# Both output gates multiplied into the weights on GpSimd, instead of into the results on VectorE

## The chip, the cores and the metric

The kernel runs on one core of a Trainium2 chip. A core has TensorE (matrix products, the rows call it PE, its weight loads PEld), VectorE (DVE), ScalarE (ACT), GpSimd (POOL) and SyncE (SP, here only a queue for transfers). Each runs its own list of instructions in order, and they meet through semaphores. The metric is the time of one execution in device microseconds; the median of several executions is compared.

## The reference

One block of a transformer with adaptive layer norms over 8 images of 256 tokens, 256 channels:

```
mod = (silu(c) @ wmod) as (8, 6, 1, 256);  sa, ca, ga, sb, cb, gb = mod[:, 0..5]
ga, gb = sign * max(|.|, 0.25)                      # the two gates, one row of 256 per image
h = layernorm(x) * (1 + ca) + sa
x = x + ga * attention(h)                           # linear attention, 16 heads, chunks of 128
h = layernorm(x) * (1 + cb) + sb
x = x + gb * (routed_moe(h) + shared(h))            # 64 experts, 6 of them per token
attention(h) ends in: rmsnorm(rmsnorm(o) * norm_w) * proj_norm_w @ ternary(proj_w).T
shared(h) = (silu(h @ ws_gate) * (h @ ws_up)) @ ws_down
```

A gate scales the columns of a projection's result. `gate * (o @ W)` equals `o @ (W * gate)` with the gate along W's columns; on this the change rests.

## The kernel before, in words

The kernel has a prologue (constants, ternary weights, modulation rows), the token loop, the expert pairs, and a last stage that sums the six expert rows of each token.

The token loop handles one image of 256 tokens per step, in two tiles of 128 tokens, and is pipelined over images by hand: in step s, TensorE projects q, k, v of image s, forms the scores and values of its two tiles, projects the attention output of image s-1 (`project_out`, L1250 to 1257), transposes the normalised x2 of image s-1 (`norm2_transpose`, L1301), computes router logits (L1310), shared gate/up (L1322), and the shared down projection of image s-2 (`shared_down`, L1331). Each engine has its own `step` function, and the order of the calls in it is the order of execution. All order is written out by hand; nothing is scheduled by a program.

VectorE's step (L995 to 1035) is: routing scores of image s-2, `shared_out(s-3)`, statistics of the next image, `shared`, `out_norms(s-1)`, routing choice, `rms`, mask of tile 0 (`mask`, L844), `state_block`, `residual(s-1)`, `norm1_apply(s+1)`, the second layer norm of image s-1 (z), mask of tile 1, slots. The two functions that the change touches:

- `residual(b)` (L821 to 835) forms x2 = x + ga * fac * projection. It waits for `fac` (the factor of both rms norms, from GpSimd) and for the projection in the PSUM bank `ps_a`. Two instructions (L829, one per tile) multiply the bank by fac and by the gate row `mod_b[:, 0]`; one (L833) adds x, which is held in `pre`. Then `norm_stats` takes statistics of x2 (L669, L674, L677). GpSimd's `power` (L421) turns the variance into rstd, VectorE applies it (L683), and TensorE's transposes wait for that.
- `shared_out(b)` (L921 to 930) forms pre = x2 + gb * shared result. One instruction (L926) multiplies the PSUM bank by the gate rows `gb_all[:, b]` into `sh_g`, a second (L929) adds x2. The expert part is multiplied by gb in the last stage (L1105), in both kernels.

GpSimd's step (L447 to 457) is: rstd of the next image's first norm, `fac`, `q_lam` (L453), rstd of the second norm, and `norm2_rows` (L433, L435), which writes the normalised rows that the experts will gather. SP loads `mod_b` for an image (L317; three rows of 256, spread over 128 partitions, two buffers) and `gb_all` once (L322). `proj_done`, `dn_done`, `h2_ready` and the like are semaphores named for what they announce.

Of the kernel before, what the change touches and what calls it, by code (L numbers as in the profile page):

```python
# [66 lines left out]
def adaln_attention_moe(nc, x, qkv_w, qkv_norm_w, proj_w, proj_norm_w, norm_w, s, gate_w, bias,  # L67
                        w_gate, w_up, w_down, ws_gate, ws_up, ws_down, c, wmod, out):
    with ExitStack() as ctx:
        def sb(name, shape, dt=F32):  # L70
            return ctx.enter_context(nc.sbuf_tensor(name, shape, dt))
# [20 lines left out]
        pick_key = sb("pick_key", [P, B, NT * TOPK], BF16)  # L92
        neg_t = sb("neg_t", [P, T])
        decay = sb("decay", [P, 4, KC, 2, T])
# [7 lines left out]
        w_qkv = sb("w_qkv", [P, KC, 3 * C])  # L102
        w_proj = sb("w_proj", [P, KC, C])
        norm_cols = sb("norm_cols", [P, KC, 3])
        q_scale = sb("q_scale", [P, 2, KC])
# [61 lines left out]
        carry = sb("carry", [P, NT, E], BF16)  # L167
        w_raw = sb("w_raw", [P, NT, E])
        w_sum = sb("w_sum", [P, NT])
        w_rec = sb("w_rec", [P, NT])  # L170
# [30 lines left out]
        wcol = [wcols[:, i:i + 1] for i in range(WBUF)]  # L201

        spare = scm[:].rearrange("p r j q t -> p (r j q t)")
        xr = ([big[:, KEYS * i:KEYS * (i + 1)] for big in (spare, decay[:].rearrange("p r j q t -> p (r j q t)"))
# [45 lines left out]
        v_taken kt_done rr_a rr2_ready eps_ready klam_ready qlam_ready kv_done state_ready sc  # L250
        mk pv o_taken os_done f5 f_ready proj_done attn_ready x2_ready ln2_ve ln2_rstd
        z2_ready h2_mul h2_ready h2t_done h2T_ready lg_done lg_exp r1 selbf_ready w_step w_ready
        carry_ready gu_done sg_exp sg1 sh_ready dn_done sh_gated pre_ready pos_done slots_ready hot_ready ramp_ready inv_done picks_added
        unramped ix_ready xtp
# [113 lines left out]
        def _(pool):  # L368
# [15 lines left out]
            g.iota(neg_left[:], pattern=[[0, 1]], base=-T, channel_multiplier=1, allow_small_or_imprecise_dtypes=True)  # L384
            g.iota(neg_t[:], pattern=[[-1, T]], base=0, channel_multiplier=0, allow_small_or_imprecise_dtypes=True)
            g.iota(part_ix[:], pattern=[[0, 1]], base=0, channel_multiplier=1)
# [40 lines left out]
            def norm2_rows(b):  # L427
# [7 lines left out]
                g.tensor_tensor(rows, rows, spread(mod_b[b % 2][:, 1], 1, NT), ALU.add).then_inc(S["h2_ready"], 1)  # L435

            def unramp_table():

                g.memset(unramp[:], 0.0).then_inc(S["c_const"], 1)
                for i, f in enumerate((1.0, -2.0, 1.0)):  # L440
                    pool.wait_ge(S["c_const"], 11 + i)
                    g.affine_select(out=unramp[:], in_=unramp[:], pattern=[[1, P]], compare_op=ALU.not_equal, fill=f,
                                    base=-i, channel_multiplier=-1).then_inc(S["c_const"], 1)

            def step(s):
# [8 lines left out]
                if s >= 1:  # L454
                    power(rstd2[:], ve2[:], 0, "ln2_ve", "ln2_rstd", s)
                    norm2_rows(s - 1)

            pool.wait_ge(S["c_lam"], 1)
# [5 lines left out]
            power(rstd2[:], ve2[:], 0, "ln2_ve", "ln2_rstd", B)  # L464
            norm2_rows(B - 1)


# [31 lines left out]
        def _(act):  # L499
# [18 lines left out]
            for j in range(KC):  # L518
                a.activation(lam_q[:, j], neg_t[:], ACT.Exp, scale=s_part[:, j:j + 1])
            a.activation(lam_rev[:], s_row[:], ACT.Exp, scale=neg_left[:, 0:1]).then_inc(S["c_lam"], 1)  # L520
# [138 lines left out]
        def _(dve):  # L659
# [161 lines left out]

            def residual(b, par, hb):

                dve.wait_ge(S["f_ready"], b + 1)
                dve.wait_ge(S["proj_done"], b + 1)
                seen(dve, S["pre_ready"], b - 1)
                dve.wait_ge(S[f"ld_modb{par}"], 16 * (hb + 1))
                for i in range(NT):
                    last = v.scalar_tensor_tensor(out=x2[par][:, i], in0=ps_a[:, C * i:C * i + C], scalar=fac[:, i:i + 1],  # L829
                                                  in1=mod_b[par][:, 0], op0=ALU.mult, op1=ALU.mult)  # L830
                last.then_inc(S["attn_ready"], 1)
                dve.wait_ge(S["attn_ready"], b + 1)
                v.tensor_tensor(x2[par][:], x2[par][:], x_all[:, NT * b:NT * b + NT], ALU.add).then_inc(S["x2_ready"], 1)  # L833
                dve.wait_ge(S["x2_ready"], b + 1)
                norm_stats(b, [x2[par][:, i] for i in range(NT)], bn2, mv2, ve2, "ln2")
# [85 lines left out]
            def shared_out(b, par):  # L921

                dve.wait_ge(S["dn_done"], b + 1)
                dve.wait_ge(S["ld_gb"], 16)
                seen(dve, S["pre_ready"], b)
                v.tensor_tensor(sh_g[:], shared_bank(b)[:, 0:NT * C].rearrange("p (i c) -> p i c", i=NT), spread(gb_all[:, b], 1, NT),  # L926
                                ALU.mult).then_inc(S["sh_gated"], 1)
                dve.wait_ge(S["sh_gated"], b + 1)
                v.tensor_tensor(pre[:, NT * b:NT * b + NT], sh_g[:], x2[par][:], ALU.add).then_inc(S["pre_ready"], 1)  # L929

# [65 lines left out]
            def step(s, par, h, hp):  # L996
# [23 lines left out]
                if has_prev:  # L1020
                    residual(s - 1, 1 - par, hp)
                if nxt:
# [18 lines left out]
            token_steps(step, B - 1)  # L1041
            par, hb = (B - 1) % 2, (B - 1) // 2
            router_scores(B - 2)
            out_norms(B - 1, par)
            shared_out(B - 3, par)
            residual(B - 1, par, hb)
            shared(B - 2)
# [65 lines left out]
        def _(pe):  # L1113
# [76 lines left out]
            def project_qkv(b):  # L1190
# [8 lines left out]
                seen(pe, S["lg_exp"], b - 1)  # L1199
                seen(pe, S["sh_gated"], b - 2)  # L1200
                seen(pe, S["state_ready"], b)
# [47 lines left out]

            def project_out(b):  # L1250
                pe.wait_ge(S["rr_a"], min(b + 2, B))
                pe.wait_ge(S["klam_ready"], min(b + 2, B))
                for i in range(NT):
                    for k in range(KC):
                        last = mm.matmul(ps_a[:, C * i:C * i + C], oT[:, i, k], w_proj[:, k],
                                        start=(k == 0), stop=(k == KC - 1))
                last.then_inc(S["proj_done"], 1)
# [46 lines left out]
            def logits(b):  # L1304
                pe.wait_ge(S["h2T_ready"], b + 1)
                seen(pe, S["state_ready"], min(b + 2, B) if isinstance(b, int) else b + 2)
                seen(pe, S["sh_gated"], min(b - 1, B - 3))
                for i in range(NT):
# [17 lines left out]
            def shared_down(b):  # L1326
                pe.wait_ge(S["sh_ready"], b + 1)
                if b < B - 3:
                    pe.wait_ge(S["lg_exp"], b + 2)
                for i in range(NT):  # L1330
                    last = mm.matmul(shared_bank(b)[:, C * i:C * i + C], s_h[:, T * i:T * i + T], ws_d[:], start=True, stop=True)  # L1331
                last.then_inc(S["dn_done"], 1)
# [156 lines left out]
```

## Time and profile before

| what | value |
| --- | --- |
| median of 3 runs | 404.2 us (401.7, 404.49, 404.2) |
| the profiled execution | 404.41 us, its span 402.7 us |
| mean granted clock of TensorE | 0.853 of full |
| TensorE matmul busy | 314.5 us (78%) |
| VectorE busy | 248.3 us (62%) |
| ScalarE busy | 134.6 us (33%) |
| GpSimd busy | 117.0 us (29%) |

The token loop fills the span from about 25 to 270 us, a step of it 27.4 us in the middle. The expert pairs run from 275 to about 347 us, and the last stage from there to the end, around transfers of `y_dram`. A busy share is an average over these stages, so what a few instructions less are worth has to be read from one step. The granted clock has two levels here, 1.00 and 0.50 of full speed; a figure between them is a mean over a stretch that holds both.

### The profile page before, as it was taken

The numbers are of one execution on the slowest core, as the hardware profiler recorded it, in microseconds if no ns is written. First come the engines' busy times: TensorE is split into PE (matmuls) and PEld (weight loads), VectorE is DVE, ScalarE is ACT, GpSimd is POOL, SyncE is SP. The second block draws the span as 40 slices with busy tenths as digits, with TensorE's granted clock in tenths as the row PEclk, the third lists the DMA queues.
The fourth block names the chain that finished last, engine by engine and source line by source line (L and its number), as shares of the span: only waits on it lengthen the run. The fifth ranks groups of instructions, "written<-read, shape, count | busy, mean of one in ns | idle before, by whom it ended". The sixth has DMA issues, their size and how long they took to land.

```text
span 402.7 us, 7088 instructions
## 1 busy us (share of the span) xinstructions
PE 314.5 (78%) x2496; PEld 234.0 (58%) x2496; DVE 248.3 (62%) x940; ACT 134.6 (33%) x368; POOL 117.0 (29%) x146
## 2 busy tenths in 40 slices
PE   3698796996987969969969975547999989407663
PEld 3584585784875857857858754434555544206552
DVE  3747327669668688698695687864555545105764
ACT  4320231331462463443613625430444434300000
POOL 5210103103202221131031033007777777720000
PEclk9999597796896996987977969655999999856998
DMA  6940699999401401413223000005699994149992
GB/s 165 337 167 3 174 330 291 261 359 253 156 25 54 158 33 41 160 57 104 71 72 132 28 33 2 33 33 110 162 271 268 267 273 123 50 191 421 402 390 81
DMA packets 52708, 65.83 MB, mean 163 GB/s; under 512 B 4446, under 2 KB 47568, under 8 KB 52672
## 3 DMA queue, kind: packets, MB, share of 16 engines
q1 hardware_dynamic: 34224, 42.66, 35.0%
q10 hardware_dynamic: 15376, 15.47, 11.0%
q0 software_dynamic: 3072, 7.25, 7.2%
q8 instruction: 20, 0.33, 0.3%
q14 instruction: 16, 0.13, 0.1%
HBM read 46.03 MB, written 21.53 MB: 168 GB/s over the span
## 4 chain that ended last, share of the span: by engine, by line
PE 41%; issue 25%; DMA 11%; DVE 10%; POOL 6%; ACT 4%; SPq 1%; POOLq 0%; DVEq 0%
DMA egu<-y_dram 5%; PE ps_a L1194 5%; PE ps_s L1438 4%; PE ps_o L1293 4%; PE ps_b L1310 4%; PE ps_c L1322 3%; DMA scm<-h_dram,tok_ix 3%; PE ps_o L1289 3%; POOL y_dram L485 3%; PE ps_b L1331 2%; PE ps_o L1246 2%; DMA decay<-h_dram,tok_ix 2%; DVE egu L1098 2%; PE ps_a L1301 2%; POOL rstd L421 2%
## 5 line engine op out<-in xcount | busy, mean ns | idle before, releaser
L421 POOL TENSOR_TENSOR rstd<-ve,half_exp 128x2 f32<-128x2 f32 x15 | 11.1, 737 | 141.6 <-DVE ve L677 141.6
L844 DVE TENSOR_TENSOR scm<-ps_s,decay 128x2048 f32<-128x2048 f32 x16 | 36.6, 2286 | 16.5 <-PE ps_s L1272 16.5
L1464 PE MATMUL ps_a<-egu,ident 128*128 128x256 f32 x48 | 13.8, 446 | 22.9 <-DVE egu L1098 22.9
L1098 DVE TENSOR_TENSOR egu<-egu 128x1536 f32<-128x1536 f32 x8 | 14.0, 1756 | 25.9 <-DMA egu<-y_dram 25.9
L549 ACT ACTIVATE h_both<-rise,place 128x128 bf16<-128x128 f32 x91 | 27.5, 402 | 6.0 <-DVE place L951 6.0
L1438 PE MATMUL ps_s<-egu,x 128*64 128x192 f32 x256 | 29.4, 351 | 0.0
L1293 PE MATMUL ps_o<-scm,v_eo 128*32 128x128 f32 x512 | 25.8, 347 | 1.0
L1464 PEld LDWEIGHTS ps_a<-egu,ident 128*128 128x128 f32 x48 | 10.5, 226 | 26.2 <-issue 18.5
L1310 PE MATMUL ps_b<-gate_sb,h2T 128*128 128x64 f32 x64 | 15.1, 414 | 8.9 <-ACT h2T L571 8.9
L1076 DVE SCALAR_TENSOR_TENSOR z<-z,ps_s 128x96 f32<-128x96 f32 x32 | 8.1, 254 | 22.3 <-ACT z L635 22.2
L1194 PE MATMUL ps_a<-h_both,w_qkv 128*128 128x256 f32 x64 | 19.3, 454 | 2.8 <-ACT h_both L529 2.8
L1301 PE MATMUL ps_a<-ident,z 128*128 128x128 f32 x32 | 6.5, 339 | 18.8 <-DVE z L683 18.8
L635 ACT ACTIVATE z<-ps_s 128x96 f32<-128x96 f32 x32 | 8.0, 251 | 39.3 <-PE ps_s L1438 39.3
L1310 PEld LDWEIGHTS ps_b<-gate_sb,h2T 128*128 128x128 f32 x64 | 13.6, 313 | 11.3 <-ACT h2T L571 11.3
L1438 PEld LDWEIGHTS ps_s<-egu,x 128*64 128x64 f32 x256 | 16.9, 141 | 5.3 <-issue 0.6
L1293 PEld LDWEIGHTS ps_o<-scm,v_eo 128*32 128x32 f32 x512 | 16.3, 134 | 6.3 <-issue 5.7
L571 ACT ACTIVATE h2T<-ps_a,mod_cols 128x256 f32<-128x256 f32 x16 | 8.2, 561 | 35.2 <-PE ps_a L1301 35.2
L1272 PE MATMUL ps_s<-qT,k_eo 32*128 32x128 f32 x512 | 18.8, 283 | 0.0
L1272 PEld LDWEIGHTS ps_s<-qT,k_eo 32*128 32x128 f32 x512 | 15.7, 186 | 4.2 <-issue 4.2
L505 ACT ACTIVATE oT<-ps_o 128x512 f32<-128x512 f32 x8 | 4.8, 597 | 36.0 <-PE ps_o L1293 36.0
L1194 PEld LDWEIGHTS ps_a<-h_both,w_qkv 128*128 128x128 f32 x64 | 13.7, 226 | 5.2 <-issue 3.2
L1206 PE MATMUL ps_b<-h_both,w_qkv 128*128 128x256 f32 x64 | 16.3, 400 | 0.0
(259 smaller groups left out, 761.2 us busy)
## 6 DMA issues: line engine op xcount, KB each, us to landing
y_dram<-y_zeros ACTq DMA_DIRECT2D x8, 1536.0 KB, 5.9
egu<-y_dram SPq DMA_DIRECT2D x16, 768.0 KB, 10.0
egu<-in_L_ffn_w_gate SPq DMA_DIRECT2D x16, 384.0 KB, 9.9
egu<-in_L_ffn_w_up SPq DMA_DIRECT2D x16, 384.0 KB, 10.7
ed<-in_L_ffn_w_down SPq DMA_DIRECT2D x16, 384.0 KB, 12.0
mod_b<-mod_dram SPq DMA_DIRECT2D x8, 384.0 KB, 3.8
h_dram<-h2row SPq DMA_DIRECT2D x8, 320.0 KB, 2.3
pre<-in_L_attn_x SPq DMA_DIRECT2D x8, 256.0 KB, 6.1
```

Source lines behind the costliest of these rows:

```text
L421: g.tensor_tensor(out_, in_, half_exp[:, which], ALU.pow).then_inc(S[done], 1)
L549: last = a.activation(ramp[:, n], rise[:], ACT.Relu, bias=place[:, n // TOPK, n % TOPK:n % TOPK + 1])
L844: v.tensor_tensor(scm[:].rearrange("p r j q t -> p (r j q t)"), ps_s[:].rearrange("p r n -> p (r n)"), decay[:].rearrange("p r j q t -> p ...
L1098: v.tensor_tensor(y[:, :, 0:3], y[:, :, 0:3], y[:, :, 3:6], ALU.add).then_inc(S["y_half"], 1)
L1194: last = mm.matmul(ps_a[:, N * j:N * j + N], w_qkv[:, k, P * j:P * j + P], hT[:, k], start=(k == 0), stop=(k == KC - 1))
L1206: last = mm.matmul(ps_b[:, N * j:N * j + N], w_qkv[:, k, C + P * j:C + P * j + P], hT[:, k], start=(k == 0), stop=(k == KC - 1))
L1272: last = mm.matmul(ps_s[:, r, col:col + T], k_eo[q][32 * r:32 * r + 32, j, ts], qT[32 * r:32 * r + 32, j, ts], start=True, stop=True)
L1293: last = mm.matmul(dst[32 * r:32 * r + 32], vq, scm[:, r, j, q], start=(q == 0 and not tile), stop=(q == 1), skip_group_check=True)
L1301: last = mm.transpose(ps_a[:, N * j + T * i:N * j + T * i + T], z2[:, i, P * j:P * j + P], ident[:])
L1310: last = mm.matmul(ps_b[:, E * i:E * i + E], h2T[:, k, T * i:T * i + T], gate_sb[:, k], start=(k == 0), stop=(k == KC - 1))
L1438: last = mm.matmul(e_gups[n][rows].rearrange("p (g f) -> p g f", f=F), xt[n][:, k, rows], egu[:, slot // 2, :, 2 * (slot % 2) + half, k], ...
L1464: last = mm.matmul(ysum[b % 2][:, C * i:C * i + C], ident[:], y[:, i, j], start=(j == 0), stop=(j == 2))
```

## The change

GpSimd gets two functions. `gate_proj(b)` multiplies the projection weights by the first gate of image b into a new tile `w_gated`, once the previous image's projection is done. `gate_shared(b)` multiplies the shared down weights by the second gate into one of two tiles that lie in `sh_g`. TensorE uses these in `project_out` and `shared_down` and waits for them (`wp_ready`, `ws_ready`). VectorE's `residual` now multiplies by fac and adds x in the same instruction, and `shared_out` is one sum. The tile `neg_t`, used only in the prologue, moves into `w_raw`, to make room. The core of the diff:

```diff
+            def gate_proj(b):
+
+                pool.wait_ge(S["q_w"], 3)
+                pool.wait_ge(S[f"ld_modb{b % 2}"], 16 * (b // 2 + 1))
+                seen(pool, S["proj_done"], b)
+                g.tensor_tensor(w_gated[:], w_proj[:], spread(mod_b[b % 2][:, 0], 1, KC), ALU.mult).then_inc(S["wp_ready"], 1)
+
+            def gate_shared(b):
+
+                pool.wait_ge(S["ld_gb"], 16)
+                pool.wait_ge(S["ld_shared"], 80)
+                seen(pool, S["dn_done"], b - 1)
+                g.tensor_tensor(ws_gated[b % 2], ws_d[:], gb_all[0:F, b], ALU.mult).then_inc(S["ws_ready"], 1)
+
...
                 if s >= 1:
                     power(rstd2[:], ve2[:], 0, "ln2_ve", "ln2_rstd", s)
                     norm2_rows(s - 1)
+                gate_proj(s)
+                if s >= 1:
+                    gate_shared(s - 1)
...
             norm2_rows(B - 1)
+            gate_shared(B - 1)
...
-                dve.wait_ge(S[f"ld_modb{par}"], 16 * (hb + 1))
                 for i in range(NT):
                     last = v.scalar_tensor_tensor(out=x2[par][:, i], in0=ps_a[:, C * i:C * i + C], scalar=fac[:, i:i + 1],
-                                                  in1=mod_b[par][:, 0], op0=ALU.mult, op1=ALU.mult)
+                                                  in1=x_all[:, NT * b + i], op0=ALU.mult, op1=ALU.add)
                 last.then_inc(S["attn_ready"], 1)
                 dve.wait_ge(S["attn_ready"], b + 1)
-                v.tensor_tensor(x2[par][:], x2[par][:], x_all[:, NT * b:NT * b + NT], ALU.add).then_inc(S["x2_ready"], 1)
-                dve.wait_ge(S["x2_ready"], b + 1)
...
-                dve.wait_ge(S["ld_gb"], 16)
-                seen(dve, S["pre_ready"], b)
-                v.tensor_tensor(sh_g[:], shared_bank(b)[:, 0:NT * C].rearrange("p (i c) -> p i c", i=NT), spread(gb_all[:, b], 1, NT),
-                                ALU.mult).then_inc(S["sh_gated"], 1)
-                dve.wait_ge(S["sh_gated"], b + 1)
-                v.tensor_tensor(pre[:, NT * b:NT * b + NT], sh_g[:], x2[par][:], ALU.add).then_inc(S["pre_ready"], 1)
+                v.tensor_tensor(pre[:, NT * b:NT * b + NT], shared_bank(b)[:, 0:NT * C].rearrange("p (i c) -> p i c", i=NT),
+                                x2[par][:], ALU.add).then_inc(S["pre_ready"], 1)
...
             def project_out(b):
+                pe.wait_ge(S["wp_ready"], b + 1)
...
             def shared_down(b):
                 pe.wait_ge(S["sh_ready"], b + 1)
+                pe.wait_ge(S["ws_ready"], b + 1)
```

Waits on `sh_gated` become waits on `pre_ready`.

On VectorE, in step 2, from the mask of tile 0 to the first statistics. Before (`x_1` is the tile x2 of image 1, `pre` holds x):

```order
L844 TENSOR_TENSOR scm<-ps_s,decay 128x2048 [waits pv,sc]
L811 TENSOR_TENSOR state<-ps_b,head_block 128x256 [waits pv,kv_done]
L829 SCALAR_TENSOR_TENSOR x_1<-ps_a,fac,mod_b 128x256 [waits ld_modb1,proj_done,f_ready]
L829 SCALAR_TENSOR_TENSOR x_1<-ps_a,fac,mod_b 128x256
L833 TENSOR_TENSOR x_1<-x_1,pre 128x512 [waits attn_ready]
L669 BN_STATS bn<-x_1 128x6 [waits x2_ready]
```

Now:

```order
L861 TENSOR_TENSOR scm<-ps_s,decay 128x2048 [waits pv,sc]
L831 TENSOR_TENSOR state<-ps_b,head_block 128x256 [waits pv,kv_done]
L848 SCALAR_TENSOR_TENSOR x_1<-ps_a,fac,pre 128x256 [waits proj_done,f_ready]
L848 SCALAR_TENSOR_TENSOR x_1<-ps_a,fac,pre 128x256
L689 BN_STATS bn<-x_1 128x6 [waits attn_ready]
```

The sum of L833 is gone, and x enters the two products instead of the gate.

On GpSimd, from the end of step 0 through step 1, as the changed kernel has it:

```order
L469 TENSOR_TENSOR q_lam<-qT,lam_q 128x256 [waits q_taken]
L444 TENSOR_TENSOR w_gated<-w_proj,mod_b 128x512 [waits ld_modb0,q_w]
L423 TENSOR_TENSOR rstd<-ve,half_exp 128x2 [waits ln1_ve]
L423 TENSOR_TENSOR fac<-fin,half_exp 128x2 [waits f5]
L469 TENSOR_TENSOR q_lam<-qT,lam_q 128x256 [waits pv,q_taken]
L423 TENSOR_TENSOR rstd<-ve,half_exp 128x2 [waits ln2_ve]
L435 TENSOR_TENSOR h2row<-z,mod_b 128x2x256 [waits ld_modb0,z2_ready]
L437 TENSOR_TENSOR h2row<-h2row,mod_b 128x2x256 [waits h2_mul]
L444 TENSOR_TENSOR w_gated<-w_proj,mod_b 128x512 [waits proj_done,ld_modb1,q_w]
L451 TENSOR_TENSOR sh_g<-ws_d,gb_all 96x256 [waits ld_shared,ld_gb]
L423 TENSOR_TENSOR rstd<-ve,half_exp 128x2 [waits ln1_ve]
```

The rows of L444 and L451 are new, the rest stands as before. The first L444 is ahead of the power of image 2, of fac and of q_lam.

## Rows read from the trace of the kernel before

**Rows 1.** The page, part 2: granted clock in 40 slices, in tenths of full.
```profile
PEclk9999597796896996987977969655999999856998
```
**Rows 2.** Waits of the whole run: who <- for whom: us in total, times, longest.
```profile
POOL rstd L421 <- DVE ve L677: 141.6, 15, 15.3
...
PE ps_a L1301 <- DVE z L683: 18.8, 8, 3.0
...
PE ps_b L1310 <- ACT h2T L571: 8.9, 8, 1.1
```
**Rows 3.** Timeline of VectorE: start us, us, line, op, tiles, [idle before <-releaser].
```profile
139.03 0.16 DVE L796 TENSOR_SCALAR rr_t<-ps_a 128x2 f32<-128x2 f32 x1 [1.28 <-PE ps_a L1218]
...
141.89 2.29 DVE L844 TENSOR_TENSOR scm<-ps_s,decay 128x2048 f32<-128x2048 f32 x1 [2.09 <-PE ps_s L1272]
...
145.47 0.69 DVE L833 TENSOR_TENSOR x<-x,pre 128x512 f32<-128x512 f32 x1
146.20 0.75 DVE L669 BATCH_NORM_STATS2 bn<-x 128x6 f32<-128x256 f32 x2
...
158.09 0.69 DVE L926 TENSOR_TENSOR sh_g<-ps_b,gb_all 128x512 f32<-128x512 f32 x1 [1.31 <-PE ps_b L1331]
```
**Rows 4.** Timeline of TensorE: transposes at three pauses, logits after one.
```profile
66.07 1.12 PE L1301 MATMUL ps_a<-ident,z 128*128 128x128 f32 x4 [2.63 <-DVE z L683]
...
149.24 0.66 PE L1301 MATMUL ps_a<-ident,z 128*128 128x128 f32 x4 [2.15 <-DVE z L683]
151.01 1.75 PE L1310 MATMUL ps_b<-gate_sb,h2T 128*128 128x64 f32 x8 [1.11 <-ACT h2T L571]
...
233.06 1.02 PE L1301 MATMUL ps_a<-ident,z 128*128 128x128 f32 x4 [2.05 <-DVE z L683]
```
**Rows 5.** Stretches: length, TensorE busy (matmuls), granted clock, transfers' share, GB/s.
```profile
147.10:151.20 4.10, 0.85 (x6) 1.00 0.21 80
151.30:158.10 6.80, 6.80 (x50) 0.50 0.22 60
...
233.30:240.00 6.70, 5.59 (x44) 0.50 0.00 1
...
376.00:397.00 21.00, 13.55 (x58) 1.00 0.82 329
...
63.40:246.10 182.70, 158.13 (x1456) 0.84 0.40 120
66.10:76.10 10.00, 8.89 (x57) 0.50 1.12 255
```
**Rows 6.** Timeline of TensorE at other places, columns as above.
```profile
155.97 2.08 PE L1331 MATMUL ps_b<-ws_d,s_h 96*128 96x256 f32 x4
...
240.24 1.13 PE L1331 MATMUL ps_s<-ws_d,s_h 96*128 96x256 f32 x4
...
276.70 0.70 PE L1427 MATMUL ps_b<-ident,scm 128*128 128x128 f32 x2 [0.93 <-DMA scm<-h_dram,tok_ix]
...
381.81 2.86 PE L1464 MATMUL ps_a<-egu,ident 128*128 128x256 f32 x12 [2.66 <-DVE egu L1098]
```
**Rows 7.** Timeline: q_lam on GpSimd, and sel_bf on VectorE twice.
```profile
136.22 0.73 POOL L453 TENSOR_TENSOR q_lam<-qT,lam_q 128x256 f32<-128x256 f32 x1 [1.17 <-ACT qT L505]
136.58 0.44 DVE L900 TENSOR_SCALAR sel_bf<-r_den 128x128 bf16<-128x128 f32 x1
...
260.95 0.23 DVE L900 TENSOR_SCALAR sel_bf<-r_den 128x128 bf16<-128x128 f32 x1
```
**Rows 8.** Users and loads of mod_b: count, ns min/median/max, first and last start.
```profile
L829 DVE SCALAR_TENSOR_TENSOR x<-ps_a,fac,mod_b x16: 473/475/484, 61.5 to 244.9; 128x256 f32<-128x256 f32 x16
L317 SPq DMA_DIRECT2D mod_b<-mod_dram x8: 325/329/1453, 41.1 to 206.8; - x8
L433 POOL TENSOR_TENSOR h2row<-z,mod_b x8: 1265/1275/1283, 66.1 to 249.1; 128x512 f32<-128x512 f32 x8
...
DMA to landing us min/median/max: 3.5/3.8/9.2
```

More of the change, by code:

```diff
@@ L92, in adaln_attention_moe @@
         pick_key = sb("pick_key", [P, B, NT * TOPK], BF16)
-        neg_t = sb("neg_t", [P, T])
         decay = sb("decay", [P, 4, KC, 2, T])
@@ L103, in adaln_attention_moe @@
         w_proj = sb("w_proj", [P, KC, C])
+        w_gated = sb("w_gated", [P, KC, C])
         norm_cols = sb("norm_cols", [P, KC, 3])
@@ L168, in adaln_attention_moe @@
         w_raw = sb("w_raw", [P, NT, E])
+        neg_t = w_raw[:].rearrange("p i e -> p (i e)")
         w_sum = sb("w_sum", [P, NT])
@@ L201, in adaln_attention_moe @@
         wcol = [wcols[:, i:i + 1] for i in range(WBUF)]
+        ws_gated = [sh_g[0:F, i] for i in range(2)]
         spare = scm[:].rearrange("p r j q t -> p (r j q t)")
@@ L250, in adaln_attention_moe @@
         v_taken kt_done rr_a rr2_ready eps_ready klam_ready qlam_ready kv_done state_ready sc
-        mk pv o_taken os_done f5 f_ready proj_done attn_ready x2_ready ln2_ve ln2_rstd
+        mk pv o_taken os_done f5 f_ready proj_done attn_ready wp_ready ln2_ve ln2_rstd
         z2_ready h2_mul h2_ready h2t_done h2T_ready lg_done lg_exp r1 selbf_ready w_step w_ready
-        carry_ready gu_done sg_exp sg1 sh_ready dn_done sh_gated pre_ready pos_done slots_ready hot_ready ramp_ready inv_done picks_added
+        carry_ready gu_done sg_exp sg1 sh_ready dn_done ws_ready pre_ready pos_done slots_ready hot_ready ramp_ready inv_done picks_added
         unramped ix_ready xtp
@@ L384, in _ @@
             g.iota(neg_left[:], pattern=[[0, 1]], base=-T, channel_multiplier=1, allow_small_or_imprecise_dtypes=True)
-            g.iota(neg_t[:], pattern=[[-1, T]], base=0, channel_multiplier=0, allow_small_or_imprecise_dtypes=True)
+            g.iota(neg_t, pattern=[[-1, T]], base=0, channel_multiplier=0, allow_small_or_imprecise_dtypes=True)
             g.iota(part_ix[:], pattern=[[0, 1]], base=0, channel_multiplier=1)
@@ L518, in _ @@
             for j in range(KC):
-                a.activation(lam_q[:, j], neg_t[:], ACT.Exp, scale=s_part[:, j:j + 1])
+                a.activation(lam_q[:, j], neg_t, ACT.Exp, scale=s_part[:, j:j + 1])
             a.activation(lam_rev[:], s_row[:], ACT.Exp, scale=neg_left[:, 0:1]).then_inc(S["c_lam"], 1)
@@ L820, in out_norms, with residual @@
                                        op0=ALU.mult, op1=ALU.add).then_inc(S["f5"], 1)
-            def residual(b, par, hb):
+            def residual(b, par):
                 dve.wait_ge(S["f_ready"], b + 1)
@@ L1020, in step @@
                 if has_prev:
-                    residual(s - 1, 1 - par, hp)
+                    residual(s - 1, 1 - par)
                 if nxt:
@@ L1041, in _ @@
             token_steps(step, B - 1)
-            par, hb = (B - 1) % 2, (B - 1) // 2
+            par = (B - 1) % 2
             router_scores(B - 2)
@@ L1045, in _ @@
             shared_out(B - 3, par)
-            residual(B - 1, par, hb)
+            residual(B - 1, par)
             shared(B - 2)
@@ L1199, in project_qkv @@
                 seen(pe, S["lg_exp"], b - 1)
-                seen(pe, S["sh_gated"], b - 2)
+                seen(pe, S["pre_ready"], b - 2)
                 seen(pe, S["state_ready"], b)
@@ L1254, in project_out @@
                     for k in range(KC):
-                        last = mm.matmul(ps_a[:, C * i:C * i + C], oT[:, i, k], w_proj[:, k],
+                        last = mm.matmul(ps_a[:, C * i:C * i + C], oT[:, i, k], w_gated[:, k],
                                         start=(k == 0), stop=(k == KC - 1))
@@ L1306, in logits @@
                 seen(pe, S["state_ready"], min(b + 2, B) if isinstance(b, int) else b + 2)
-                seen(pe, S["sh_gated"], min(b - 1, B - 3))
+                seen(pe, S["pre_ready"], min(b - 1, B - 3))
                 for i in range(NT):
@@ L1330, in shared_down @@
                 for i in range(NT):
-                    last = mm.matmul(shared_bank(b)[:, C * i:C * i + C], s_h[:, T * i:T * i + T], ws_d[:], start=True, stop=True)
+                    last = mm.matmul(shared_bank(b)[:, C * i:C * i + C], s_h[:, T * i:T * i + T], ws_gated[b % 2], start=True, stop=True)
                 last.then_inc(S["dn_done"], 1)
```

## The prediction

> **What bounds the kernel now.** I read the page first, then the waits of the whole run, then the timeline of one step of the token loop, image by image, and last the clock of chosen stretches. The page's shares name no engine that is full. They do say that TensorE's clock is granted only in part: its line swings between 9 and 6 tenths through the token loop, and never rests at 9 there [rows 1]. The waits say who makes whom wait [rows 2]: TensorE's transposes at L1301 waited 18.8 us for VectorE's z, eight times, and the logits at L1310 waited 8.9 us for ScalarE's h2T, eight times. GpSimd sat idle 141.6 us for VectorE's ve, so it has room.
>
> The timeline shows the place [rows 3]. In the step that starts near 133 us VectorE has nothing to do before 141.89 (it had waited 2.09 us for the scores). From there it runs without a gap: mask, state, the two projection products at 144.57, the sum with x at 145.47 (0.69 us), the statistics at 146.20, GpSimd's power, z. TensorE gets its transposes at 149.24 after 2.15 us of idleness, works 0.66 us, and stands another 1.11 us until the logits at 151.01 [rows 4]. Elsewhere in the step TensorE has no pause longer than a few tenths. So each of the eight images has one **double pause** of TensorE, 3.3 us idle within 3.9 us, and its first half ends with VectorE's chain from the scores to z. That chain is the only place where less VectorE work moves the end.
>
> The pause costs twice. Up to 151.2 the granted clock is 1.00; from 151.3 to 158.1 it is 0.50, the 1.2 GHz level instead of the 2.4 GHz one, with TensorE busy all of those 6.8 us [rows 5]. The shared down projection, which lies in such a stretch, took 2.08 us there and 1.13 us at 240.24, where the clock was up again [rows 6]. So 6.8 us at the low level cost about 3.4 us. After each of the eight pauses comes such a low stretch, of 6.8 us or, as from 66.1 to 76.1, of 10 [rows 5]. The eighth, before the last image's logits, lies where VectorE's routing is the bound, and the clock is worth little.
>
> **The change part by part.**
> *Residual.* The two scalar_tensor_tensor products stay, with x as their second tensor in place of the gate (0.475 us each, [rows 8]; same shapes, one operand in PSUM as before): 0. The sum at L833 goes, once an image, 8 in all: 0.69 us. From its start at 145.47 to the start of the statistics at 146.20 is 0.73 us with the wait between [rows 3]. Everything behind it moves up by that, and so do z and the transposes. 8 x 0.73 = **5.8 us**, all of it on the path, since the pauses before the transposes (18.8 us over eight) are longer than 0.73 each.
> *Shared output.* One 0.69 us product of two goes. Before it VectorE stands 1.31 us waiting for the down projection, and behind it VectorE waits again, 1.28 us for rr_t and 2.09 us for the scores [rows 3]. The 0.7 us only lengthens those idle times: **0**. The last two stand ahead of the first expert pair, but TensorE then waits for the gathered rows of the second pair until 276.70 [rows 6], whatever VectorE does: 0 (bounds: 0 to 2 x 0.69 = 1.4 us gained).
> *GpSimd.* It gains the projection weights' product, the same shape as L433, 1.27 us [rows 8], and the shared weights' product, 96x256, at most the 0.73 us of q_lam, 128x256 [rows 7]: 2.0 us an image, 16 in all, directly after norm2_rows. What follows there in its queue is a power that waits for ve. Nothing is queued behind them that is late. They are needed one step later (project_out) or later still (shared_down). 0.
> *Step 0.* The first product stands in GpSimd's queue before the power of image 2, fac of image 0 and q_lam of image 1, and it waits for the load of mod_b, issued at 41.1 us; landings take 3.5 to 9.2 us [rows 8], so it is through by 41.1 + 9.2 + 1.3 = 51.6. The first user of fac starts at 61.5 [rows 8]. Cover: 10 us. 0.
> *TensorE, SP.* The same matmuls from other tiles, one more wait each; loads and stores in the same order: 0.
> *The shared port.* While GpSimd ran q_lam (136.22 to 136.95) VectorE's sel_bf took 0.44 us, against 0.23 us at 260.95, where GpSimd was idle [rows 7]. So GpSimd's work does hold up some VectorE operations. The new 2.0 us fall on slots and router_scores. At worst VectorE stands for all 2.0 us; idle behind it in the same step are 1.31 + 1.28 + 2.09 = 4.7 us, plus the 0.7 us saved. I take 0, and keep 0.5 us an image (4 us) as an end of the range, for steps where faster TensorE work has used up that idle time.
>
> The Trainium skill (SBUF, State Buffer; "Who interferes with whom") speaks against the change here: a VectorE instruction with two SBUF inputs and a GpSimd one that reads SBUF exclude one another, and the later fully blocks. The row above agrees in kind. By the page the whole 2.0 us could be lost each time, which is the worst case already taken.
>
> *The clock.* This is the large term, and the trace doesn't show a double pause of the new size. It will be 1.43 us idle, 0.66 busy, 1.11 idle. Bounds: no low stretch vanishes (0), or all seven on the TensorE-bound part do: from 63.4 to 246.1 the mean clock is 0.84, so (1 - 0.84) x 2 x 182.7 = 58 us are low, TensorE is busy in all but 3 or 4 of them [rows 5], and half of that is 27 us. Between them: at three of the eight (the first is 66.07, the last 233.06) the transposes themselves took 1.02 to 1.12 us instead of 0.66 [rows 4], so the clock had fallen during the first pause, after some 2.0 to 2.6 us of idleness. The new first pause is over after 1.4 us. On the other side a pause of 2.66 us between full groups of matmuls, at 381.81 [rows 6], left the clock at 1.00, as did all of 376 to 397 with TensorE busy 13.55 of 21 us [rows 5]. So the old pause lies near the edge, a fall depends on where it comes, and 2.5 us of idleness instead of 3.3 should be spared sometimes. I take those three as spared. Two are long, 8.9 us of work, one short, 5.6 us [rows 5]: (2 x 8.9 + 5.6) / 2 = **11.7 us**. Which ones they are I can't say: steps get shorter, and the pauses move against whatever decides.
>
> The Trainium skill (TensorE: Matmul & The Clock Gate, "What's actually happening") says that this monitor runs freely, not reset by the kernel. By it the same pause may cost a low stretch or not, and the number spared would differ between runs.
>
> Sum: -5.8 - 11.7 = -17.5. The profiled execution took 404.4 us (span 402.7 and 1.7 around it), beside a median of 404.2: **387 us**.
>
> **The rivals.**
> *A. The clock falls as often as before.* For it: eight falls in eight pauses. Against it: 2.66 us without one. -5.8 us: 398.6.
> *B. Nearly all low stretches vanish.* Then VectorE must keep up with a step of some 23 us; a step takes it 27.4 us, less 4.7 idle and 1.4 removed is 21.3, so it would. 404.4 - 5.8 - 27 = 372.
> *C. Slower: the low stretches get longer.* Lengths of 6.8 and 10.2 us both occur. If moved pauses make the four TensorE-bound short ones long, each costs 1.7 us, 6.8 in all, against 5.8 gained: 405.4. From the fourth lengthened stretch on it is slower than before; past 1% it would need more than two further ones. Nothing in the profile favours that direction.
> *D. GpSimd's products reach the path.* 0.5 us an image with the falls unchanged: -5.8 + 4 = 402.6. It decides only where VectorE's 4.7 us of idleness are gone. That needs the clock to stay up, which then pays for it.
> *E. The change doesn't do what it says,* because the first product comes late: over 10 us of cover speak against it.
>
> **How the numbers follow.** A measurement of this kernel tells a change from none at about 1%, 4 us. Forecast (two to five stretches spared, 380 to 394): 0.50. A: 0.22. B (below 380): 0.13. D and other losses that leave 400 to 408: 0.10. C and worse: 0.05, most of it still within 1%. Leaving out the lower part of B (0.08) and what is above 401 (0.12), the range is **378 to 401**. The forecast's own range is 380 to 394. Faster by over 1%: 0.50 + 0.22 + 0.13 = 0.85. Same 0.12, slower 0.03.
>
> **What the changed profile would show.** L833 and L926 gone; the projection products with pre among their inputs, the statistics 0.04 us behind them. The wait of the transposes for z at about 18.8 - 5.8 = 13 us over eight. GpSimd's busy time up by 16 us, its idle time for ve down by about as much. VectorE's busy time down by 11 us. Fewer than eight low stretches between 60 and 260 us, steps of about 23.3 us where there is none, 26.7 where it lasts 6.8. The last stages, from the first expert pair on, as long as before. It would be wrong if low stretches follow every shortened pause (A), or if mask or rr_t no longer waits for TensorE (D).

## The result, and the profile after

| what | before | after |
| --- | --- | --- |
| median of 5 runs | 404.2 us | 393.3 us (389.8 to 395.02) |
| ratio, with its 95% interval | | 0.972 [0.968, 0.976] |
| the profiled execution, its span | 404.41, 402.7 us | 389.8, 388.1 us |
| clock granted to TensorE, mean | 0.853 | 0.867 |

The change saves 10.9 us, where 17 were forecast; 393.3 lies inside the stated range of 378 to 401. A ratio is taken from the fast executions of either kernel alone, so where some were slower (over 1.5% above the fastest) it is not the quotient of the two medians. The profiled execution is the shortest of its five, so its trace shows some 3.5 us more gain than the median. Of the changed kernel's page, part 1 and the clock of part 2:

```profile
PE 307.1 (79%) x2496; PEld 228.1 (59%) x2496; DVE 243.6 (63%) x924; ACT 134.7 (35%) x368; POOL 132.4 (34%) x162
...
PEclk9999579798995899979969987556999999856999
```

GpSimd is busier by 15.4 us, as expected. VectorE's busy time fell by 4.7 us only, not 11. The clock's line still dips in the token loop [rows 1]. Waits of the whole run, who <- for whom, us in total, times, longest:

```profile
POOL rstd L423 <- DVE ve L697: 99.8, 13, 10.9
...
DVE scm L861 <- PE ps_s L1286: 16.1, 8, 2.1
...
PE ps_a L1315 <- DVE z L703: 13.3, 8, 2.2
...
PE ps_b L1324 <- ACT h2T L591: 8.9, 8, 1.1
```

The transposes' wait for z fell from 18.8 to 13.3 us [rows 2], and VectorE still waits for the scores. Its timeline in the step that answers to [rows 3]:

```profile
137.94 2.29 DVE L861 TENSOR_TENSOR scm<-ps_s,decay 128x2048 f32<-128x2048 f32 x1 [2.09 <-PE ps_s L1286]
140.28 0.42 DVE L831 TENSOR_TENSOR state<-ps_b,head_block 128x256 f32<-128x256 f32 x1
140.62 0.87 DVE L848 SCALAR_TENSOR_TENSOR x<-ps_a,fac,pre 128x256 f32<-128x256 f32 x2
141.52 0.75 DVE L689 BATCH_NORM_STATS2 bn<-x 128x6 f32<-128x256 f32 x2
...
143.77 0.74 DVE L703 TENSOR_SCALAR z<-x,mv,rstd 128x256 f32<-128x256 f32 x2 [0.36 <-POOL rstd L423]
```

From the mask to the statistics it is 141.52 - 137.94 = 3.58 us, where it was 146.20 - 141.89 = 4.31: the 0.73 us of the sum. Now TensorE's transposes at three images, and the logits after one, which answer to [rows 4]:

```profile
91.19 0.66 PE L1315 MATMUL ps_a<-ident,z 128*128 128x128 f32 x4 [2.16 <-DVE z L703]
...
144.56 0.66 PE L1315 MATMUL ps_a<-ident,z 128*128 128x128 f32 x4 [1.43 <-DVE z L703]
146.33 0.88 PE L1324 MATMUL ps_b<-gate_sb,h2T 128*128 128x64 f32 x6 [1.11 <-ACT h2T L591]
...
168.13 0.66 PE L1315 MATMUL ps_a<-ident,z 128*128 128x128 f32 x4 [1.43 <-DVE z L703]
```

The double pause has the forecast size: 1.43 idle, 0.66 busy, 1.11 idle. All eight transposes take 0.66 us, so in this execution the clock never falls in the first half any more. It falls in the second half instead, or within about 1.1 us of the logits' start. Stretches of the token loop: length, TensorE busy, granted clock, transfers' share, GB/s; the first row is the whole stretch from the first transposes to the last (the row of before is 66.07:249.09 with 0.84), then pieces of it, and last everything behind the token loop:

```profile
65.12:235.22 170.10, 149.95 (x1452) 0.89 0.42 124
...
94.20:97.40 3.20, 3.20 (x37) 0.50 1.14 233
118.10:128.10 10.00, 10.00 (x58) 0.50 0.16 42
144.60:168.10 23.50, 20.85 (x232) 1.00 0.28 99
169.20:175.80 6.60, 5.90 (x46) 0.50 0.22 62
...
256.30:388.10 131.80, 97.19 (x582) 0.88 0.75 230
```

One image of the eight, that of 144.56, has no low stretch; the step there is 168.13 - 144.56 = 23.57 us. Two stretches are short, about 3.4 us (from 94.1 and 223.8), the other four behind the first seven images as long as before, 6.8 or 10.2 us. The one behind the last image runs on past the loop. From the first transposes to the last it is 170.10 us where it was 183.02. The low stretches behind the first seven images add up to 3 x 6.8 + 10.2 + 2 x 3.4 = 37 us, where the prediction had counted 58 before.

### The profile page after: what moved, and what is told of

Same layout as the page of the kernel before. It is cut to its first block, busy times and chain, and to the rows that moved or that the text cites. A ratio compares the mean times of both kernels' runs of the same rounds, so it can differ in the third digit from the quotient of the medians.

```text
span 388.1 us, 7093 instructions
## 1 busy us (share of the span) xinstructions
PE 307.1 (79%) x2496; PEld 228.1 (59%) x2496; DVE 243.6 (63%) x924; ACT 134.7 (35%) x368; POOL 132.4 (34%) x162
## 4 chain that ended last, share of the span: by engine, by line
PE 31%; issue 20%; DVE 14%; SPq 13%; DMA 11%; POOL 7%; ACT 3%; POOLq 0%; DVEq 0%
PE ps_s L1453 5%; DMA egu<-y_dram 5%; SPq L333 5%; SPq L334 5%; SPq L332 3%; POOL y_dram L505 3%; PE ps_a L1207 2%; PE ps_o L1307 2%; DMA decay<-h_dram,tok_ix 2%; DVE egu L1111 2%; PE ps_b L1324 2%; PE ps_c L1336 2%; PE ps_c L1466 2%; PE ps_b L1479 1%; PE ps_b L1442 1%
## 5 line engine op out<-in xcount | busy, mean ns | idle before, releaser
L1111 DVE TENSOR_TENSOR egu<-egu 128x1536 f32<-128x1536 f32 x8 | 14.1, 1756 | 25.9 <-DMA egu<-y_dram 25.9
L1324 PE MATMUL ps_b<-gate_sb,h2T 128*128 128x64 f32 x64 | 12.6, 360 | 8.9 <-ACT h2T L591 8.9
L1286 PE MATMUL ps_s<-qT,k_eo 32*128 32x128 f32 x512 | 18.8, 283 | 0.0
L444 POOL TENSOR_TENSOR w_gated<-w_proj,mod_b 128x512 f32<-128x512 f32 x8 | 10.3, 1286 | 23.3 <-DMA mod_b<-mod_dram 15.7
L1324 PEld LDWEIGHTS ps_b<-gate_sb,h2T 128*128 128x128 f32 x64 | 11.2, 263 | 10.8 <-ACT h2T L591 10.8
```

What stands on the lines that cost most here:

```text
L1111: v.tensor_tensor(y[:, :, 0:3], y[:, :, 0:3], y[:, :, 3:6], ALU.add).then_inc(S["y_half"], 1)
L1286: last = mm.matmul(ps_s[:, r, col:col + T], k_eo[q][32 * r:32 * r + 32, j, ts], qT[32 * r:32 * r + 32, j, ts], start=True, stop=True)
L1324: last = mm.matmul(ps_b[:, E * i:E * i + E], h2T[:, k, T * i:T * i + T], gate_sb[:, k], start=(k == 0), stop=(k == KC - 1))
```

## The experiments

The further kernels were timed in three groups, each on a chip of its own together with the kernel before, which took 402.6 us (17 runs) on the first, 427.2 (17 runs) on the second and 427.7 (7 runs) on the third. Kernels of different groups are therefore compared by ratio, or by the token loop. The end of the loop is taken as the one GpSimd instruction on `pool_pad` between the loop and the experts; it starts at 270.36 us in the profile of before and at 256.30 after.

### The pauses filled, with and without the change

Both kernels got idle matmuls in both halves of the double pause, into a part of `ps_b` that is free there; nothing uses them. The kernel before has `sh_gated` where the changed one has `pre_ready`.

```diff
+            def filler(b, n):
+                seen(pe, S["state_ready"], min(b + 2, B))
+                seen(pe, S["pre_ready"], min(b - 1, B - 3))
+                for _ in range(n):
+                    mm.matmul(ps_b[:, C:2 * C], w_qkv[:, 0, 0:P], w_qkv[:, 0, 0:C], start=True, stop=True)
 def norm2_transpose(b):
+                filler(b, 2)
...
 def logits(b):
+                filler(b, 2)
```

The kernel before with it:

> The kernel before, with two idle matmuls of 128x256 (about 0.95 us at the full clock) put into each half of TensorE's double pause, ahead of the waits for z and for h2T. Their results are read by nobody. Theory (the pause costs its own length plus the low clock behind it): the low stretches between 60 and 246 us go, which were 58 us long; 404 - 27 = about 377 us, 385 at the most if some stay; the waits for z fall by about 0.95 us each without moving the steps. Rival (the pauses alone cost, the clock does not matter): 404 us or a little more.

Measured: 378.1 us (377.4 to 379.1), ratio 0.939 [0.934, 0.944], and the loop's end at 245.32. The changed kernel with it:

> The changed kernel with the same filling of the pauses. Theory: with the clock up in both, only the 0.73 us per image are left between the two kernels: 5.8 us below the filled kernel before, about 371 us. Rival 1 (the clock was not the reason why the gain of the change was 11 and not 6 us): 11 us below the filled kernel before. Rival 2 (a fast step is bound by VectorE or by GpSimd's two products): as fast as the filled kernel before, or slower.

Measured: 373.9 us (371.1 to 374.7), ratio 0.929 [0.924, 0.933], the loop's end at 238.61. The loop's clock from the first transposes to the last, without the change, and with it:

```profile
66.29:224.75 158.46, 145.95 (x1508) 1.00 0.45 134
```

```profile
62.97:217.53 154.56, 146.10 (x1509) 1.00 0.48 142
```

No low stretch is left there in either. With no work removed, the filled kernel before gains 24.5 us. So the low stretches follow from TensorE's pauses, and the whole clock term was worth about what the upper bound said (27 us). The two also show the residual term by itself. Transposes of neighbouring images, before and changed, both filled:

```profile
162.56 0.65 PE L1309 MATMUL ps_a<-ident,z 128*128 128x128 f32 x4 [1.21 <-DVE z L683]
186.86 0.66 PE L1309 MATMUL ps_a<-ident,z 128*128 128x128 f32 x4 [1.21 <-DVE z L683]
```

```profile
157.17 0.65 PE L1323 MATMUL ps_a<-ident,z 128*128 128x128 f32 x4 [0.48 <-DVE z L703]
180.73 0.66 PE L1323 MATMUL ps_a<-ident,z 128*128 128x128 f32 x4 [0.48 <-DVE z L703]
```

Steps of 24.30 and 23.56 us: 0.74 us less, in the wait for z. Over all steps between first and last transposes it is 158.46 - 154.56 = 3.9 us, since the first two steps and the last gain less (0.35, 0.27 and 0.37); the medians differ by 4.2. The loops' ends differ by more, 6.7 us, but 3.3 of that lie ahead of the first transposes, where the clock was low for 13.7 us in one trace and for 3.4 in the other.

### One part of the change alone

The residual part alone: w_gated on GpSimd, and x in place of the gate on VectorE.

```diff
+                gate_proj(s)
...
-                                                  in1=mod_b[par][:, 0], op0=ALU.mult, op1=ALU.mult)
+                                                  in1=x_all[:, NT * b + i], op0=ALU.mult, op1=ALU.add)
...
-                v.tensor_tensor(x2[par][:], x2[par][:], x_all[:, NT * b:NT * b + NT], ALU.add).then_inc(S["x2_ready"], 1)
```

> Only the first gate is multiplied into the projection weights; the shared output keeps its two VectorE products. Theory: this is the whole gain, 391 to 395 us (404.2 - 5.8 - 5 of clock), the same as the full change within 1%. Rival (VectorE's total work counts): half of the gain, about 399 us.

Measured: 393.3 us (391.8 to 395.3), ratio 0.978 [0.973, 0.983], beside 0.972 [0.968, 0.976] of the whole change: nearly all of its gain. Its first five pauses are those of the changed kernel within 0.1 us. In its trace two of the first seven images have no low stretch. The shared part alone:

```diff
+                    gate_shared(s - 1)
...
-                v.tensor_tensor(sh_g[:], shared_bank(b)[:, 0:NT * C].rearrange("p (i c) -> p i c", i=NT), spread(gb_all[:, b], 1, NT),
-                                ALU.mult).then_inc(S["sh_gated"], 1)
```

> Only the second gate is multiplied into the shared down weights; the residual keeps its sum. Theory: 0.7 us a step less on VectorE where it waits for TensorE anyway: 404 us, within 1% of before. Rival (VectorE's total work counts): about 399 us.

Measured: 405.5 us (398.7 to 407.4, 12 runs), ratio 0.999 [0.992, 1.006]. Eight VectorE instructions of 0.7 us fewer, and nothing gained. The ratio rests on three of the twelve runs, and the median is 2.9 us above the 402.6 of the kernel before, so a small loss isn't excluded.

### GpSimd's product without its use

The kernel before, with the projection weights multiplied on GpSimd, and the result left unused:

```diff
+                g.tensor_tensor(w_gated[:], w_proj[:], spread(mod_b[b % 2][:, 0], 1, KC), ALU.mult).then_inc(S["wp_ready"], 1)
...
+                gate_proj(s)
```

> The kernel before, in which GpSimd makes the gated projection weights once per image as in the change, and nobody uses them; VectorE and TensorE do what they did. It prices GpSimd's work and the blocking on the shared port alone. Theory: the product of L940 is held up about 1 us by it in each step, in time that VectorE had idle; 403 to 405 us, within 1% of before. Rival (the blocking reaches the path): 0.5 to 1 us per image more, 407 to 412 us.

Measured: 425.7 us beside 427.2, ratio 1.000 [0.994, 1.006]. The product does hold up VectorE. The group of the routing product (count | busy, mean ns), first of the kernel before, then of this one:

```profile
L940 DVE TENSOR_TENSOR keep<-keep,row_key 128x128 f32<-128x128 f32 x8 | 2.3, 290 | 0.0
```

```profile
L949 DVE TENSOR_TENSOR keep<-keep,row_key 128x128 f32<-128x128 f32 x8 | 7.6, 949 | 0.0
```

That is 5.3 us more on VectorE, and the loop ends where it did:

```profile
270.36 0.20 POOL L425 TENSOR_TENSOR pool_pad<-half_exp 128x1 f32<-128x1 f32 x1 [18.63 <-DVE tok_ix L990]
```

```profile
270.45 0.19 POOL L426 TENSOR_TENSOR pool_pad<-half_exp 128x1 f32<-128x1 f32 x1 [18.66 <-DVE tok_ix L999]
```

The second trace is of this run, the first of the kernel before. The same routing product in the changed kernel, behind the GpSimd instruction that it meets:

```profile
118.82 1.30 POOL L444 TENSOR_TENSOR w_gated<-w_proj,mod_b 128x512 f32<-128x512 f32 x1
```

```profile
118.92 1.34 DVE L953 TENSOR_TENSOR keep<-keep,row_key 128x128 f32<-128x128 f32 x1
...
125.29 0.69 DVE L941 TENSOR_TENSOR pre<-ps_b,x 128x512 f32<-128x512 f32 x1 [0.46 <-PE ps_b L1346]
```

It starts 0.10 us behind the GpSimd product and ends 0.14 us behind its end. VectorE still comes to a wait for TensorE 5 us further on.

### Which half of the pause brings the clock down

The changed kernel with the filler in one half only.

```diff
 def norm2_transpose(b):
+                filler(b, 2)
```

> The changed kernel, with two idle matmuls in the first half of each double pause only (ahead of the wait for z). Idleness left: some 0.5 and 1.1 us. Theory (a fall needs both halves together, since all falls of the changed kernel came after the second half): the low stretches go, 372 to 377 us. Rival (the second half alone is enough): 385 to 393 us, stretches as before.

```diff
 def logits(b):
+                filler(b, 2)
```

> The changed kernel, with two idle matmuls in the second half of each double pause only (ahead of the wait for h2T). Idleness left: 1.4 and some 0.2 us. Theory: the low stretches go as well, 372 to 377 us. Rival (the first half is what counts, the change has only shortened it too little): 385 to 393 us.

The change itself on the same chip:

> The changed kernel itself once more, to see how its own low stretches fall in another execution. Theory (a shortened pause may or may not bring the clock down, by where it comes): again 390 to 395 us, with low stretches at some images and not at the same ones, or of other lengths. Rival (it is fixed by the program): the same stretches to 0.1 us.

Measured: first half filled 401.6 us (ratio 0.947 [0.939, 0.955]), second half filled 402.5 us, four runs from 395.1 to 409.4 and too scattered for a ratio, the change itself 414.5 (0.971 [0.960, 0.983]). The loops tell them apart. First half filled, then second, then the change itself:

```profile
64.93:228.35 163.42, 149.38 (x1480) 0.94 0.46 130
```

```profile
65.44:219.65 154.21, 139.63 (x1480) 1.00 0.48 138
```

```profile
64.51:238.35 173.84, 154.03 (x1453) 0.86 0.46 125
```

The change itself has six falls behind the seven images on this stretch, as in the first trace. At the first image here the clock fell at 64.8, during the transposes, behind a first half of 1.91 us; so the change does not keep every fall out of the first half:

```profile
64.51 0.87 PE L1315 MATMUL ps_a<-ident,z 128*128 128x128 f32 x4 [1.91 <-DVE z L703]
```

With 0.48 us left of the first half (0.85 and 1.21 at the first two images) and all of the second the clock still fell after four of the seven images. With the first half whole and 0.24 us left of the second it never fell there, though what is idle over the eight images is nearly the same (6.2 + 8.9 us against 13.9 + 1.7). One trace is little for that, so the filled second half ran again on a third chip, beside both halves filled and beside a smaller dose:

```diff
 def logits(b):
+                filler(b, 1)
```

> The changed kernel with two idle 256-column matmuls in the second half of the pause alone (between the transposes and the logits), which an earlier run showed without a low stretch in the token loop. Their results are used by nothing. Theory (the second half decides, since every fall of the changed kernel came behind it): the token loop is again free of low stretches from 60 to 215 us, its steps 23.6 us, its end at 241 us, whatever the chip, and the whole beats the change alone by 15 to 20 us (ratio to the kernel before on the same chip about 0.935). Rival (the run before was luck; only the idle sum of the two halves counts, and filling either is worth the same): three or four falls come back and the loop ends near 249, as with the first half filled.

> The changed kernel with two idle matmuls in each half, as in the fastest run so far, beside the version that fills the second half alone. Theory (second half decides): the same loop as with the second half filled but for the start, within 3 us, so that two of the four idle matmuls do nothing. Rival (idle sum counts): 8 to 10 us faster than that one.

> As the version that fills the second half of the pause of the changed kernel, with one idle matmul in place of two: the 1.11 us before the logits have then about 0.6 us idle. Theory (second half decides, by its length): falls mostly vanish still, the loop ends by 245 us. Rival (any idleness of this size brings the clock down): four or more falls, the loop ends at 250 or later.

Measured: second half 396.6 us, ratio 0.930 [0.922, 0.937]; both halves 396.6 us, 0.933 [0.926, 0.941]; one matmul in the second half 402.1 us from runs of 396.5, 396.7, 407.5 and 409.3, no ratio. The ratio with the second half filled, 0.930 [0.922, 0.937], and that with the first half filled, 0.947 [0.939, 0.955], don't overlap, though the chips differ. The loops end at 241.14, 240.99 and 243.21. The second half alone, and one matmul in it:

```profile
65.75:219.86 154.11, 139.57 (x1481) 1.00 0.47 138
```

```profile
64.85:221.94 157.09, 139.52 (x1467) 0.98 0.46 135
66.50:73.10 6.60, 6.48 (x49) 0.50 1.12 251
```

The pause with the one matmul, at an image behind which the clock stayed up (L1316 is the filler; its one call stands as x2, as the two calls in another row stood as x4):

```profile
138.02 0.66 PE L1322 MATMUL ps_a<-ident,z 128*128 128x128 f32 x4 [1.43 <-DVE z L703]
138.51 0.60 PE L1316 MATMUL ps_b<-w_qkv 128*128 128x256 f32 x2
139.78 0.43 PE L1332 MATMUL ps_b<-gate_sb,h2T 128*128 128x64 f32 x2 [0.68 <-ACT h2T L591]
```

Some 0.4 us less idleness, with 1.43 and 0.68 us still idle, and five of the change's six falls are gone; the one that is left comes at the first image. The second half is not all, though. At the eighth pause, whose first half is longer, the clock fell in all three traces with only the second half filled, before the logits had started. The second such trace, with 6.8 us at the low level from 221.2:

```profile
219.86 0.66 PE L1322 MATMUL ps_a<-ident,z 128*128 128x128 f32 x4 [2.64 <-DVE z L703]
221.62 1.97 PE L1332 MATMUL ps_b<-gate_sb,h2T 128*128 128x64 f32 x8 [0.22 <-ACT h2T L591]
```

Filling the first half as well adds nothing to the loop. The changed kernel with its second half filled is the version to keep; with both halves filled, the fastest that was timed on the first chip (373.9 us), it is as fast.

## Why the prediction held, and where it was off

**Residual, 5.8 us: right in kind, slightly too large.** The wait for z fell by 5.5 us, 0.73 in each steady step. Where the clock hides nothing, the two filled kernels differ by 3.9 us in the loop and 4.2 in the median. The part alone gives nearly the gain of the whole change.

**Shared output, 0: right within the noise.** The part alone has ratio 0.999. At the first expert pair up to 1.4 us had been left open. The first product of the pair waited for VectorE's sum in the kernel before:

```profile
275.07 0.70 PE L1427 MATMUL ps_a<-ident,scm 128*128 128x128 f32 x2 [1.51 <-DVE pre L929]
```

Now TensorE waits for gathered rows there, as at the second product:

```profile
260.48 0.67 PE L1442 MATMUL ps_a<-ident,scm 128*128 128x128 f32 x2 [0.99 <-DMA scm<-h_dram,tok_ix]
...
262.33 0.70 PE L1442 MATMUL ps_b<-ident,scm 128*128 128x128 f32 x2 [1.18 <-DMA scm<-h_dram,tok_ix]
```

From the loop's end to that second product it is 6.03 us where it was 6.34, so of the 1.4 us some 0.3 came in this trace.

**GpSimd and step 0, 0: right.** Its busy time grew by 15.4 us. The first product:

```profile
43.65 1.27 POOL L444 TENSOR_TENSOR w_gated<-w_proj,mod_b 128x512 f32<-128x512 f32 x1 [15.67 <-DMA mod_b<-mod_dram]
...
47.85 0.69 POOL L423 TENSOR_TENSOR fac<-fin,half_exp 128x2 f32<-128x2 f32 x1 [2.28 <-DVE fin L839]
```

It ends at 44.92, 6.7 us before the bound of 51.6, and fac comes long before its first user. Rival E is out.

**The shared port, 0: right in time, with a miss in its sign.** I had VectorE's busy time fall by 11 us. 11.0 us of instructions did go, but keep takes 5.3 us more, and a few small routing operations take up to 2 us more, which the run with the unused product doesn't show. The product made and unused costs no time beyond the noise of 0.6%, and in the filled kernels, where no low clock gives cover, the steps still differ by the full 0.74 us. So rival D is out there too. The Trainium skill (SBUF, State Buffer; "Who interferes with whom") says that the later of two such instructions fully blocks; keep, with 1.34 us instead of 0.29, agrees.

**The clock, 11.7 us: this step failed in its size.** I had reasoned from the three transposes of 1.02 to 1.12 us: there the clock had fallen in the first half of the pause, the change shortens that half, so these three low stretches would be spared. The first half did get shorter, and the conclusion did not hold. In the profiled execution no fall comes in the first half, but the same pause still has a second half of 1.11 us, which the change doesn't touch, and the fall comes there or shortly behind instead. (The second trace of the changed kernel has one, at its first image.) Three falls were put off, not spared. One image went without, and two low stretches shrank to about 3.4 us. The trace of before held a sign of this: at the other five images the transposes took 0.66 us and the clock fell in the second half or within 0.4 us of the logits' start, as at 151.3 behind logits that started at 151.01 [rows 4, 5]. Only the three falls in or ahead of the transposes had been priced. The experiments agree: with the second half filled, the falls behind the first seven images all vanish, with first halves of 1.33 to 2.16 us left; with the first half filled, four stay.

By the medians the clock gave 10.9 - 5.8 = 5 us, and 3.5 us in the residual part alone (9.3 - 5.8). In the profiled execution it is more: the loop ends 270.36 - 256.30 = 14.1 us earlier, 8.6 beyond the 5.5 of the wait. On the second chip it came to 12.7 - 5.8 = 7. So by the medians it was a third to three fifths of what I took, between the forecast and rival A. The low time agrees: 58 - 37 = 21 us less of it in the profiled execution, at the 0.40 to 0.46 us that a low microsecond cost (below), are 8 to 10 us, beside the 8.6 measured. That 393.3 still falls into the forecast's own 380 to 394 is partly luck: that part of the range stood for two to five spared stretches, and one was spared.

Rival A (fell as often: 398.6) comes closer in the count of falls, since seven of eight pauses still had one, than in time; it left out that they can get shorter. Rival B (372) needed the second half of the pause, which this change cannot reach; that is what the filled kernel got, 373.9. Rival C's longer stretches did occur (10 us from 118.1, where it had been 6.8), but shorter ones outweighed them. (Two further lengthened stretches, not more than two, would have passed 1% there: 405.4 + 2 x 1.7 = 408.8, where 1% is 408.4.)

**Steps and last stages.** A step without a low stretch took 23.57 us instead of the 23.3 forecast, one with 6.8 us of it 26.3 instead of 26.7. So 6.8 us at the low level cost 2.7 to 3.1 us, not 3.4 (in the kernel before, 27.42 - 24.30 = 3.1): part of the step goes by other engines. Behind the loop the changed kernel took 131.80 us and the kernel before:

```profile
270.36:402.70 132.34, 95.86 (x582) 0.87 0.75 229
```

The gain was made in the loop, as promised.

**That what is spared differs between executions.** In either trace of the changed kernel one image of the first seven had no fall, that of 144.56 in one and that of 170.03 in the other. The Trainium skill (TensorE: Matmul & The Clock Gate, "What's actually happening"), with its monitor that runs freely, agrees with this. Other traces don't show it. The kernel before was traced once, but the run with the unused product, whose TensorE work is the same, has its low stretches from 60 to 281 us within 0.1 us of those. So has the residual part alone its first five beside the changed kernel's.

**Open.** Why a first half of 1.33 to 2.16 us is harmless when the second is filled, while one of 2.64 us is not, nor a second half of 1.11 us when the first is cut to 0.5. Whether the 0.66 us of transposes between the halves count as work like the idle matmuls wasn't tested, and the first half alone was filled in one trace only. And what makes some low stretches short: in the two traces of the changed kernel the three short ones start 0.9 to 1.1 us behind the start of the logits, the nine others behind the first seven images at most 0.3 us behind it, or before. That says which ones are short, not why.

## What to carry to other kernels

Where TensorE's clock drops behind a pause, price the pause as a whole: look for the piece of it that stays when your change has cut the rest. Before counting on a better clock from shorter waits, put idle matmuls into each piece of the pause alone; that is a few lines, it tells in one run what the clock is worth, and here it was worth twice the change itself. An operand may be scaled on an engine that has room, even where that blocks another for a microsecond, as long as the blocked one waits again in the same step.

## What the runs showed of the hardware

- One idle fp32 matmul of 256 columns per image between transposes and logits, which left 0.68 us idle there instead of 1.11, left one low stretch behind the first seven images where the change alone has six. Two of them, in both halves or in the second alone, left none in each of five traces, on three chips.
- With only the second half filled and a first half of 2.64 us, the clock fell all the same, from 221.2 for 6.8 us; with 2.16 us and less it stayed up.
- Low stretches of about 3.4 us occur (94.20:97.40 at 0.50), beside those of 6.8, 10.2 and more in the kernel before.
- A GpSimd product of 1.30 us stretched a VectorE product of 0.29 us to 1.34 us where the two met (all eight of them from 2.3 to 7.6 us), and the time of the kernel did not change (1.000 [0.994, 1.006]).
- The kernel before took 402.6 us on one chip and 427.2 on another. It wasn't traced on the second; the run with the unused product was, and its token loop ends within 0.1 us of the other trace (270.45 and 270.36). The difference lies behind the loop, in 150.25 us instead of 132.34, at a granted clock of 0.81 instead of 0.87. The changed kernel itself shows the same, with 152.08 us there instead of 131.80. First the run with the unused product, then the changed kernel, both on the second chip:

```profile
270.45:420.70 150.25, 108.22 (x582) 0.81 0.63 202
```

```profile
259.62:411.70 152.08, 112.99 (x582) 0.77 0.63 199
```
